# Second cross attention of a gated transformer: the rows for the experts normalised on ScalarE, half of the second softmax lowered by its maximum on GpSimd

## The reference

```python
x = x + jnp.tanh(g_xattn[0]) * _L0_xattn_ref(_layernorm(x), ctx, ctx, ...)
x = x + jnp.tanh(g_ffn[0])   * _L0_ffn_ref(_layernorm(x), ...)          # six layers
x = x + jnp.tanh(g_xattn[1]) * _L1_xattn_ref(ctx, _layernorm(x), ...)   # this one is changed
x = x + jnp.tanh(g_ffn[1])   * _L1_ffn_ref(_layernorm(x), ...)          # experts
```

```python
attn = softmax(einsum('bhnd,bhmd->bhnm', q, k) * SCALE)      # 16 heads of 8
gate = 0.5 * mean(x @ w_la) + 0.5 * max(x @ w_la)            # one number per sequence and head
attn2 = softmax(gate * attn)
out = einsum('bhnm,bhmd->bnhd', w * attn2 + (1 - w) * attn, v)
return out @ w_proj + b_proj
```

## Time and profile before

| | us |
|---|---|
| median of 3 runs (lowest to highest) | 4179.61 (4177.51 to 4183.59) |
| the profiled execution | 4172.27 |
| its span, first to last instruction | 4170.4 |
| TensorE busy in the span | 3973.7 (95%) |
| VectorE busy | 3509.2 (84%) |
| ScalarE busy | 3006.3 (72%) |
| GpSimd busy | 2884.2 (69%) |

### The profile page before, as it was taken

One profiled execution on the slowest core, in us unless ns is written; L12 is line 12 of the kernel. 1 busy time (PEld: TensorE's weight loads), 2 busy tenths in 40 slices (PEclk: granted clock), 3 DMA queues, 4 the chain that ended last, 5 costly groups with the idle time before them and its releaser, 6 DMA issues.

```text
span 4170.4 us, 147277 instructions
## 1 busy us (share of the span) xinstructions
PE 3973.7 (95%) x50345; PEld 2760.5 (66%) x50345; DVE 3509.2 (84%) x7187; ACT 3006.3 (72%) x6843; POOL 2884.2 (69%) x3647
## 2 busy tenths in 40 slices
PE   5999998999999999999999999999999999799899
PEld 3777775666666666666666666666666666566665
DVE  4666667899998998899988999889999999688876
ACT  2555556888888888788887888888888888566522
POOL 2333336888887888788887888888888888567500
PEclk9999999999999999999999999999999999899999
DMA  3000001000000001000010000100000000000000
GB/s 91 6 8 6 8 4 49 9 9 8 25 21 9 10 8 30 17 7 10 7 35 12 7 10 18 27 9 9 9 25 21 8 10 7 15 15 14 7 10 10
DMA packets 162233, 64.89 MB, mean 16 GB/s; under 512 B 121556, under 2 KB 156128, under 8 KB 162016
## 3 DMA queue, kind: packets, MB, share of 16 engines
q1 hardware_dynamic: 162016, 62.05, 5.9%
HBM read 26.54 MB, written 2.10 MB: 7 GB/s over the span
## 4 chain that ended last, share of the span: by engine, by line
POOL 42%; PE 27%; issue 23%; DVE 5%; POOLq 2%; ACT 1%; SPq 1%; DVEq 0%; DMA 0%; ACTq 0%
POOL qn L651 11%; POOL qn L640 8%; POOL big L651 7%; POOL e L646 6%; POOL big L640 4%; PE pj L1631 3%; PE pp L1589 2%; PE po L1604 2%; PE sc L2000 2%; PE pj L1623 2%; PE po L1915 2%; PE pj L1672 1%; POOL rstd L662 1%; PE po L1610 1%; PE turn L1575 1%
## 5 line engine op out<-in xcount | busy, mean ns | idle before, releaser
L1698 PE MATMUL pj<-wqkv,xcT 128*128 128x512 f32 x1536 | 799.8, 603 | 17.1 <-issue 8.9
L651 POOL TENSOR_TENSOR qn<-qn,big 128x512 f32<-128x512 f32 x384 | 491.4, 1280 | 292.7 <-DVE big L1213 292.7
L863 ACT ACTIVATE big<-pj 128x512 f32<-128x512 f32 x768 | 473.9, 617 | 67.8 <-PE pj L1698 57.4
L1213 DVE TENSOR_TENSOR big<-pj,ropes 128x512 f32<-128x512 f32 x768 | 521.5, 679 | 0.0
L1219 DVE TENSOR_REDUCE ss<-big 128x8 f32<-128x512 f32 x768 | 514.9, 671 | 0.2 <-ACT big L863 0.2
L651 POOL TENSOR_TENSOR big<-big 128x512 f32<-128x512 f32 x384 | 485.8, 1275 | 4.8 <-DVE big L1213 4.8
L1851 PEld LDWEIGHTS pp<-wo,oT 128*128 128x128 f32 x3072 | 357.3, 191 | 161.1 <-issue 81.0
L646 POOL TENSOR_TENSOR e<-e,rc 128x512 f32<-128x512 f32 x384 | 400.9, 1044 | 54.2 <-DVE rc L1243 54.2
L640 POOL TENSOR_TENSOR qn<-qn,ny 128x512 f32<-128x512 f32 x384 | 397.1, 1044 | 7.5
L640 POOL TENSOR_TENSOR big<-big,ny 128x512 f32<-128x512 f32 x384 | 397.0, 1045 | 7.6
L1851 PE MATMUL pp<-wo,oT 128*128 128x128 f32 x3072 | 393.9, 281 | 1.6 <-ACT oT L886 1.2
(11 more groups left out here) (321 smaller groups left out, 9863.0 us busy)
## 6 DMA issues: line engine op xcount, KB each, us to landing
wqkv<-in_L_ffn_Wqkv SPq DMA_DIRECT2D x18, 512.0 KB, 3.6
xsd<-Y SPq DMA_DIRECT2D x192, 32.0 KB
xsd<-Y SPq DMA_DIRECT2D x384, 15.8 KB
xsf<-Y SPq DMA_DIRECT2D x96, 64.0 KB
xsf<-Y SPq DMA_DIRECT2D x192, 31.5 KB
xsx<-Y SPq DMA_DIRECT2D x64, 64.0 KB, 1.8
xsx<-CT SPq DMA_DIRECT2D x64, 64.0 KB, 1.9
wo<-in_L_ffn_Wo SPq DMA_DIRECT2D x6, 512.0 KB, 4.4
```

Of the source, the lines that this page charges most:

```text
L651: nc.gpsimd.tensor_tensor(U[a.par][i], U[a.par][i], t2b[i % 2], ALU.add).then_inc(sem("d_add"), 1)
L863: nc.scalar.activation(sqb[i % 2], pj[i % 2][:, :], ACT.Square).then_inc(sem("d_sq"), 1)
L1213: nc.vector.tensor_tensor(t2v, swapped, sin, ALU.mult).then_inc(sem("d_r"), 1)
L1698: mm(pj[i % 2][:, :], xcT[:, a.par, :], wqkv[:, i * 512:i * 512 + 512], start=True, stop=True).then_inc(sem("d_ch"), 1)
```

## The change

Two pieces of work move from VectorE to other engines, in the second cross attention alone.

- `normalise` is now ScalarE's: one activation, row times inverse deviation plus a bias, called for `p[6]` at the head of ScalarE's round. The bias, minus mean times inverse deviation, is a new step of GpSimd (`bias_of_mean`, for `p[4]`, at the end of its round), with a new semaphore `l_nb` that ScalarE waits for. In the last rounds ScalarE calls it for the last tiles, and VectorE's routing steps are no longer cut in two.
- The subtraction of the maximum from the second half of the second softmax (`sub2(p[3], 1)`) is now GpSimd's (`below_max`), placed between the two masked key rows. It has a semaphore of its own, `l_sb3`, for which `exp2(p[3], 1)` waits on ScalarE, and the next tile's `max2` on VectorE.
- The gate's sum on GpSimd counts on the semaphore `l_g1` in place of a second one. TensorE's code and SyncE's are unchanged.

```diff
+                def below_max(tile):
+                    if tile:
+                        past(pool, "l_mx2", tile.g * 2 + 2)
+                        v = by_head(l_e2[tile.par % 2][1])
+                        nc.gpsimd.tensor_tensor(v, v, bc(h8(mx, 1, 1), S), ALU.subtract).then_inc(sem("l_sb3"), 1)
...
+                def bias_of_mean(tile):
+                    if tile:
+                        past(pool, "norm_nr", tile.g * 2 + (NR0 + 2))
+                        past(pool, "l_y", tile.g - 3)
+                        past_waits(pool, "went_on")
+                        nc.gpsimd.tensor_scalar(n_nb[:, 0, tile.par:tile.par + 1], n_mean(tile.par), n_rstd(tile.par, 1), -1.0, ALU.mult, ALU.mult).then_inc(sem("l_nb"), 1)
...
                 key_rows_masked(p[1], 0)
+                below_max(p[3])
                 key_rows_masked(p[1], 1)
...
                 gate_sum(p[1])
+                bias_of_mean(p[4])
...
                 def exp2(tile, h):
                     if tile:
-                        past(act, "l_sb2", tile.g * 2 + (h + 1))
+                        past(act, "l_sb3" if h else "l_sb2", tile.g + 1)
...
+                def normalise(tile):
+                    if tile:
+                        past(act, "l_res", tile.g + 1)
+                        act.wait_ge(sem("l_nb"), tile.g + 1)
+                        past_waits(act, "went_on")
+                        nc.scalar.activation(r_in[tile.par % 2], X[:, tile.t, :], ACT.Identity, scale=n_rstd(tile.par, 1), bias=n_nb[:, 0, tile.par:tile.par + 1]).then_inc(sem("l_y"), 1)
+
+                ending = p[3] is None and p[6] is not None
+                if not ending:
+                    normalise(p[6])
                 tile_turned(p[1])
...
-                def normalise(tile):
-                    if tile:
-                        past(dve, "norm_nr", tile.g * 2 + (NR0 + 2))
-                        nc.vector.tensor_scalar(r_in[tile.par % 2], X[:, tile.t, :], n_mean(tile.par), n_rstd(tile.par), ALU.subtract, ALU.mult).then_inc(sem("l_y"), 1)
...
-                if not ending:
-                    normalise(p[6])
                 inverse1(p[3])
...
                 gate_stats(p[1])
-                sub2(p[3], 1)
                 residual(p[4])
```

More of the change, by code:

```diff
@@ L278, in build @@
         FIRST = NT - MT
+        n_nb = sb("n_nb", [P, 1, 4])
         r_one = {n: sb("r_" + n, [P, NT]) for n in ("max", "sum", "inv", "top", "rank")}
@@ L595, in _ @@
             nc.gpsimd.memset(l_la[:, :], 0.0).then_inc(sem("l_la0"), 1)
-            head_start(pool, "norm_nr", "z_x", "l_ga", "l_os", "l_km", "l_xb", "l_z", "x_p", "d_un", "d_pr", "d_add", "d_nt", "f_eps", "f_rstd")
+            head_start(pool, "norm_nr", "z_x", "l_ga", "l_os", "l_km", "l_xb", "l_z", "l_sb3", "x_p", "d_un", "d_pr", "d_add", "d_nt", "f_eps", "f_rstd")
             nc.gpsimd.memset(xsd[:, :, :], 0.0)
@@ L733, in gate_sum @@
                         i = tile.par % 2
-                        pool.wait_ge(sem("l_g1"), tile.g + 1)
-                        nc.gpsimd.tensor_tensor(l_gm[:, i, 0:2], l_gm[:, i, 0:2], l_gm[:, i, 2:4], ALU.add).then_inc(sem("l_g2"), 1)
+                        pool.wait_ge(sem("l_g1"), tile.g * 2 + 1)
+                        nc.gpsimd.tensor_tensor(l_gm[:, i, 0:2], l_gm[:, i, 0:2], l_gm[:, i, 2:4], ALU.add).then_inc(sem("l_g1"), 1)
                 def gate_rows(tile):
@@ L739, in gate_rows @@
                         i = tile.par % 2
-                        pool.wait_ge(sem("l_g2"), tile.g + 1)
+                        pool.wait_ge(sem("l_g1"), tile.g * 2 + 2)
                         past(pool, "l_P1", tile.g - 1)
@@ L796, in _ @@
         def _(act):
-            head_start(act, "r_c", "l_Vc", "l_xc", "l_kq", "l_ex1", "l_ex2", "l_C1", "l_C2", "l_oc", "x_xc", "x_e", "x_c0", "x_oc", "d_xc", "d_sq", "d_cl", "d_ln", "d_rn", "d_vc", "d_tc", "d_e", "d_mk", "d_pc", "d_oc", "f_gl", "f_xT")
+            head_start(act, "r_c", "l_y", "l_Vc", "l_xc", "l_kq", "l_ex1", "l_ex2", "l_C1", "l_C2", "l_oc", "x_xc", "x_e", "x_c0", "x_oc", "d_xc", "d_sq", "d_cl", "d_ln", "d_rn", "d_vc", "d_tc", "d_e", "d_mk", "d_pc", "d_oc", "f_gl", "f_xT")
             act.wait_ge(s_ld, NLOAD)
@@ L1041, in l_step @@
                 if p[3] and isinstance(p[3].g, int) and p[3].g == NT - 1:
+                    normalise(p[5])
                     act.wait_ge(sem("r_st"), 2)
                     nc.scalar.activation(r_buf[0][:, 0:FIRST, :], r_buf[0][:, 0:FIRST, :], ACT.Exp).then_inc(sem("r_e"), 1)
+                if ending and p[4]:
+                    normalise(p[5])
+                    normalise(p[4])
                 exp1(p[1], 0)
@@ L1093, in normalise_input @@
                         nc.vector.tensor_scalar(Y[:, k, :], X[:, k, :], mean[:, bass.ds(k, 1)], rstd[:, bass.ds(k, 1)], ALU.subtract, ALU.mult).then_inc(sem("n_t"), 1)
-            head_start(dve, "norm_st", "norm_ag", "z_ready", "l_y", "l_gs", "l_c1", "l_rc1", "l_t1", "l_t2", "l_mx1", "l_mx2", "l_sb1", "l_sb2", "l_res", "x_ev", "x_m", "x_r", "x_c1", "x_res", "d_r", "d_ss", "d_mx", "d_sub", "d_sm", "d_rc", "d_res",
+            head_start(dve, "norm_st", "norm_ag", "z_ready", "l_gs", "l_c1", "l_rc1", "l_t1", "l_t2", "l_mx1", "l_mx2", "l_sb1", "l_sb2", "l_res", "x_ev", "x_m", "x_r", "x_c1", "x_res", "d_r", "d_ss", "d_mx", "d_sub", "d_sm", "d_rc", "d_res",
                        "f_xn", "f_hT", "f_st", "f_ag", "f_mv")
@@ L1375, in max2 @@
                         past(dve, "l_z", tile.g * 2 + (h + 1))
+                        if h:
+                            past(dve, "l_sb3", tile.g)
                         nc.vector.tensor_reduce(h8(mx, 1, h), by_head(l_e2[tile.par % 2][h]), AX, ALU.max).then_inc(sem("l_mx2"), 1)
@@ L1412, in aggregate @@
                         nc.vector.bn_aggr(dif[:, 16 + 2 * tile.par:18 + 2 * tile.par], n_st(tile.par)).then_inc(sem("norm_ag"), 1)
-                def normalise(tile):
-                    if tile:
-                        past(dve, "norm_nr", tile.g * 2 + (NR0 + 2))
-                        nc.vector.tensor_scalar(r_in[tile.par % 2], X[:, tile.t, :], n_mean(tile.par), n_rstd(tile.par), ALU.subtract, ALU.mult).then_inc(sem("l_y"), 1)
-                ending = p[3] is None and p[6] is not None
-                if not ending:
-                    normalise(p[6])
                 inverse1(p[3])
@@ L1439, in l_step @@
                 if p[3] and isinstance(p[3].g, int) and p[3].g == NT - 1:
-                    normalise(p[5])
                     route(0, 7)
[L1442 to L1446, removed]
+                if p[4] and isinstance(p[4].g, int) and p[4].g == NT - 1:
+                    route(7, ROUTE_STEPS)
             tt, reduce, stt = nc.vector.tensor_tensor, nc.vector.tensor_reduce, nc.vector.scalar_tensor_tensor
```

## The result

The changed kernel takes **4264.2 us** (median of 4 runs, 4257.1 to 4266.9); the kernel before took 4178.6 beside it (4 runs, 4175.4 to 4183.6). The ratio is 1.0202, with a 95% interval of 1.0189 to 1.0215: 86 us slower. The forecast was 4218, its range ended at 4236. The direction was right, the size was less than half of what came.

The account below looks back on a forecast made before the run. A round was taken as TensorE's own order plus its waits for ScalarE. 22 x 1.34 + 5 x 1.08 = 34.9 us, plus head 1 and tail 2, gave 38 us on a median of 4179.6: 4218, range 4206 to 4236.

Parts of the forecast that it names:

- The order that cannot be overtaken: Scores, maximum, subtraction, exponential, ScalarE's normalisation, then TensorE's group with the row's turn, which starts 1.35 us later.
- The terms of a full-speed round: Row's turn 3.8 us after the scores' start, normalisation 0.46, three GpSimd steps of 1.03: round 10.45 us, 1.37 more.
- The two hand-overs to TensorE: From ScalarE's normalisation to the row's turn 0.1 us; from GpSimd's second key row to the scores 0.07 us.
- the step: Loss over 27 rounds of the second cross attention: 22 x 1.34 + 5 x 1.08 = 34.9 us.
- The loop's seam: Five rounds where a new loop turn begins; TensorE already stood still 0.83 us there, so the loss is 1.08.
- GpSimd's part by itself: GpSimd's subtraction between key rows without ScalarE's term: round 9.10 us, 0.03 more; total 4182 as a rival, chance 0.05.
- the two paths: To the next scores: 10.43 us through ScalarE's row and exponential, 10.45 through GpSimd's key rows; neither covers the other.
- VectorE: Rival that VectorE was the bound: 1.7 us freed each round makes the kernel 15 us faster, 4165; chance 0.04.
- The clock: Rival: TensorE falls to half speed, 1.3 us a hit; 4235 if every second round, 4253 if every round; chance 0.13.
- The sum: 34.9 us for 27 rounds, 1 for the head, 2 for the tail: 38 us more, total 4218.
- Head and tail: Two rounds before the 27, without rows to normalise, 1 us for both; the stage's last rounds, 2 us.
- The listed sign of the clock: In the profile after, score matmuls taking 1.9 us in many rounds would mean that TensorE's clock had fallen.

Follow-up runs that it names:

- e3: The changed kernel with ScalarE's normalisation of the next round's row ahead of its last copy instead of behind its exponential: 4190.5 us, ratio 1.0026.
- e5: The changed kernel with ScalarE's normalisation ahead of its copy of the turned second half and GpSimd's subtraction back on VectorE: 4189.5 us, ratio 1.0016.
- e12: The changed kernel with 4 products of a constant 128x128 tile on TensorE ahead of its wait for the row: 4237.3 us, ratio 1.0127.
- e1: The kernel before with only the second half's subtraction moved to GpSimd, between the key rows; VectorE still normalises: 4182.4 us, ratio 1.0008.
- e2: The changed kernel with the subtraction back on VectorE; ScalarE still normalises at the head of its round: 4252.1 us, ratio 1.0176.
- e7: The changed kernel with ScalarE normalising ahead of its copy of the turned second half and GpSimd subtracting behind both key rows: 4191.0 us, ratio 1.0026.
- e6: The kernel before with the second half's subtraction on GpSimd behind both key rows; VectorE still normalises: 4180.5 us, ratio 0.9992.
- e9: The kernel before with ScalarE copying the turned second half twice, first into a spare tile: 4198.9 us, ratio 1.0048.
- e10: The kernel before with ScalarE copying the turned second half three times, two of them into spare tiles: 4211.3 us, ratio 1.0078.
- e4: The changed kernel with 14 turns of a constant tile on TensorE ahead of its wait for the row: 4234.3 us, ratio 1.0128.

## Why the prediction was right in direction and wrong in size

**The order that cannot be overtaken: right.** Scores, maximum, subtraction, exponential (S + 2.70, as in the earlier trace rows), normalisation 0.53 later, L1962. e3 and e5 show that the place is all: half a microsecond of new work on ScalarE costs the stage nothing where ScalarE had idled.

**The terms of a full-speed round: right in kind, a little short.** The normalisation took 0.48 us (0.46 predicted). The two hand-overs to TensorE were what I had too small: from the normalisation's end (3802.80) to L1962 0.25 us instead of 0.1, from the second key row's end (3811.13) to the scores 0.25 instead of 0.07. I had taken them from pairs in the earlier trace rows, the shortest at hand. Three steps on GpSimd took 3.04 instead of 3.1. With the row later by 0.16 (S + 3.96) that makes 10.45 + 0.16 + 0.18 - 0.06 = 10.73, and e12's regular rounds are 10.73. Over the 27 rounds the wait is 40.8, where the step said 34.9. (The loop's seam lies in six of the 27 rounds, where I counted five; by my own terms that is 0.3 us less.)

**GpSimd's part by itself: right in the total, which can't tell so little from nothing.** 4182 for that path alone, 4182.4 measured (e1); but its rounds are 9.21, not 9.10, by the same hand-over to the scores (0.23 instead of 0.07). That the two paths end close to each other held within 0.2 us: 10.43 and 10.45 predicted, 10.55 without (e2) and 10.73 with GpSimd's step (e12).

**VectorE: right.** Its relief is worth nothing (e7), it waits instead.

**The clock: the step that failed.** The sum puts it at nothing, and I gave the rival 0.13, with "Against: TensorE has work again at once after each" as the reason. That is no reason: in the rows above L1962 starts as soon as the row is there and the low clock shows in the group behind it or about a microsecond later. What the sum left out measured 38.2 us, against 40.8 for the wait that it had. The evidence was in the earlier trace rows, where one of two stops of 2.09 us was followed by half speed; a stop of that length in *every* round should have had the larger chance. My prices were near: 1.3 us a hit (1.5 measured), "every round 4253" for the total. That rival happened, on top of a wait that is 6 us longer. The Trainium skill, page "TensorE: Matmul & The Clock Gate", section "HAM oscillation — how this bites in real kernels", tells of a kernel that is thrown back to the low clock by a wait in every turn of its loop. Its waits are of some 3 to 5 us; the trace shows the same pattern in 25 rounds of 27 with stops of 2.06.

**Head and tail.** Head 1.0, as predicted. Tail 5.5 instead of 2; but e6, which leaves ScalarE as it was, has 253.8 from its last scores to the end too, against 249.5 before, so I can't say that the change made these. The 4.7 us ahead of the stage were in no step, and the runs of before alone spread over 26 us (4162 to 4189).

**The tests named in the prediction.** Turn of the row released by the normalisation after about 1.9 us: yes (2.06). Three steps of 1.03 in a row on GpSimd: yes. VectorE idle over 2.5 us a round: yes (over 4 in the round above). Scores 10.3 to 10.6 us apart: no, 11.2 to 13.1 in the slow rounds, and 10.73 in e12, where the clock held. The listed sign of the clock, scores of 1.9 us, would have misled: none of the 27 rounds has them, since the low clock sits behind the stop and is over by then. The sign is in the groups right behind the stop.

## What to carry to other kernels

Where an engine works in order, the first place in its round is the latest for what the previous round's data already allow: a step whose inputs are long there belongs where that engine idles, ahead of its own wait, and not at the head of the order. Price a wait on TensorE twice, by the time it stands still and by the speed behind it: here they cost 41 and 38 us. To tell the two apart, put harmless work into the stop and see what time comes back.

## What the runs showed of the hardware

A stop of 2.0 to 2.3 us in each round of 10 to 11 us at full speed took TensorE to 1.2 GHz in 16 to 25 rounds of 27, for part of the round each, though it worked without a pause of over 0.6 us for the rest; stops of 1.0 and 1.5 us (e9, e10) did so in 6 and 5, stops of 0.55 us in none to two. Adding work to TensorE made the kernel 30 us faster (e4). Four constant products ahead of the stop left no slow round, seven constant turns left 7; the stops behind them differ by 0.13 us (1.17 and 1.30), and fourteen turns left 3 behind a stop of only 0.54 (e4); how much of this is due to the kind of work stays open, as does why of stops of equal length some are followed by the low clock and some not.
